# Second attention of a two-layer cross-attention and experts kernel: the shared experts' second product in token-major form

## The chip, the cores and the metric

One core of one Trainium2 chip. The metric is the device time of one execution in microseconds (us). Most executions of a kernel agree within 0.3%, and about 1% is what a comparison of medians of this kernel can tell from no change.

## What is computed

The input is 32 tiles of 128 tokens with 128 features. Two layers follow each other, each a cross-attention with a residual and a mixture of experts with a residual. The change touches the second layer alone. Its attention is a linear one (softmax over the 8 features of a head of queries and keys, then products with a summed key-value matrix); its experts' part has eight routed experts, of which each token takes two, and two shared experts that every token takes:

```
sh     = gelu(einsum('td,sdh->sth', xf, sW1) + sb1)        # s = 2 shared experts, h = 512
shared = (einsum('sth,shd->std', sh, sW2) + sb2).mean(axis=0)
gates  = xf @ rW + rb                                      # top 2 of 8, softmax over the two
moe    = sum over the two chosen experts of w * (gelu(xf @ W1[e] + b1[e]) @ W2[e] + b2[e])
x      = x + shared + moe
```

xf is the layer norm of the residual stream after the attention. All arithmetic that matters here is float32; the routing's counts and ranks are products of bfloat16 zeros and ones.

## The kernel before

Each engine has one hand-written queue of instructions; semaphores (`S("name")`) tie them together. The order in each queue is the order of the source. The kernel runs through five stages: the first attention (to about 240 us), the first routed experts (to about 400), the second attention with the shared experts woven in (about 404 to 615), the second routed experts, and the additions of their results.

**Second attention.** The 32 tiles are done in eight groups of four (`NGRP` = 8, `GT` = 4). On TensorE the loop is `for u in range(NGRP + 2)` at L1775: iteration u has group u's attention, group u-1's routing and, between them, the two shared experts for earlier groups. The latter come as `fill(k, ...)`: `half(u, k)` (L1692) turns k = 0 to 15 into one half of a shared chunk, an even k an up product (`shared_up`), an odd k a down product (`shared_down`, L1714). A group has eight chunks (`NC1S` = 8: two experts, four slices of 128 hidden units), so there are 64 chunks in all; the first down product of group g stands at k = 11 of iteration g+1, its last at k = 9 of iteration g+2.

TensorE's order in iteration u: turn the normed input; fill 0, 1; queries; fill 2, 3; `expert_turned(u-1)` (turns `xa`, the input of the experts); fill 4, 5; `exps_turned(u)`; `logits(u-1)`; fill 6, 7; `values(u)` (the numerators `nums`, in banks 2 and 3); fill 8, 9; `column_sums(1, u-1)`; fill 10; `out_turned(u)`; fill 11; `ranks(1, u-1)`; fill 12; `project(u)`; `shared_turn(u-2)`; fill 13 to 15.

**The shared experts' second product.** The hidden activations `hS` lie with hidden units on the partitions and the group's 512 tokens along them. `shared_down` takes the weights (128 x 128) as the stationary operand and streams the 512 tokens, so the result is features by tokens, summed over eight chunks in bank 6. ScalarE's `shared_out` (L828 to 834) halves it, adds the bias (`sb2`, one value for each partition) and puts it into `yS`; `shared_turn` (L1717) turns it into token-major form in bank 7 with four transposes, and VectorE's `shared_add` (L1052) adds it to the residual stream `x_sb`.

**Routing.** For each group VectorE's `choose` (L886) picks two experts from the logits, `column_sums` and `ranks` (L1363, L1369) on TensorE count and rank the choices, VectorE's `sums` (L911) copies the column sums out of PSUM between them and `slots` (L928) makes row numbers; GpSimd scatters the rows (L554) and makes the inverse deviations (`inverse_std`, L529). For layer 1 column sums and ranks use bank 7 (`rank_bank`), which they share with the turned shared result. After the last group VectorE's `block_list` (L949) writes `e_i`, from which the sync queue (L445 to L458) fetches weights and rows for each block of the routed experts.

**ScalarE** in iteration u (L836 to L867): copy of the turned input; gelu(0); `keep_input(u-1)` (L664 into `xa`); gelu(2); exponentials of the queries (L847); copy of the turned `xa` into `xeT_all` (a call of `turned`); gelu(4); copy of the turned exponentials; gelu(6); normed input of the next group; gelu(8); `shared_out(u-2)`; gelu(10); copy of the turned output; gelu(12), gelu(14). Gelu and the exponential need different tables; the program that builds the instructions puts in ACT_TABLE_LOADs, which have the line of the activation that they precede.

**VectorE** in iteration u (L1299 on): bias and moments, query, additions of the first experts' results, `shared_add(u-3)`, logits and `choose` for u-1, `output(u)` (L1277, four long instructions), `sums`, `gates`, `slots` for u-1, residual and moments of u. The shared bias is summed once ahead of group 0 (`shared_bias`, L1239). `link` makes VectorE wait for the instruction before.

## Time and profile before

| what | value |
|---|---|
| median of 3 runs | 783.42 us (781.82 to 787.84) |
| the profiled execution | 779.32 us |
| its span in the trace | 777.3 us |
| TensorE busy | 685.8 us, 88% |
| VectorE busy | 465.3 us, 60% |
| ScalarE busy | 326.5 us, 42% |
| GpSimd busy | 382.0 us, 49% |
| shared down products, L1714 | 128 passes, 65.4 us |
| shared result on ScalarE, L833 | 8 of 687 ns |

How to read it: the busy shares are means over stages that have different limits. A float32 product is seen as two MATMUL passes. A pass's length in the timeline has a modelled end and overlaps with the next, so what a product costs is read from the start of one to the start of the next. PE is TensorE's matmul, PEld its weight load, DVE VectorE, ACT ScalarE, POOL GpSimd, SP SyncE.

### The profile page before, as it was taken

To read this page: it belongs to the slowest core of one execution; us is meant where nothing else is said; L and a number is where in the kernel's file an instruction comes from. 1 tells how busy PE (TensorE), PEld (TensorE's weight loads), DVE (VectorE), ACT (ScalarE), POOL (GpSimd) and SP (SyncE) were. 2 spreads that over 40 slices of the span, in tenths; PEclk is the share of its full clock that TensorE was granted. 3 is DMA by queue.
4 is the path that set the end of the run, shared out by engine and by line. 5 is a ranking of instruction groups with operands and counts; after the bars stand their busy time and mean duration, and the time that the engine had idled before them with its cause. 6 is when DMAs were issued, how large, how long until landed. Compare 5 with 4: busy or idle time off the path is not lost.

```text
span 777.3 us, 15729 instructions
## 1 busy us (share of the span) xinstructions
PE 685.8 (88%) x5140; PEld 505.9 (65%) x5140; DVE 465.3 (60%) x1348; ACT 326.5 (42%) x689; POOL 382.0 (49%) x502
## 2 busy tenths in 40 slices
PE   7989999999898968899878799999999689999990
PEld 3556666667666668788776445555544289999990
DVE  4556877787677667776547766667553423333326
ACT  3434455445333232222212466666764244444440
POOL 5213176566537624556561365555555425545552
PEclk9999999999889789999987899999999999999995
DMA  6811111221101567777663000000000578877669
GB/s 165 251 22 9 10 32 22 31 30 25 33 10 36 127 175 235 236 227 234 196 212 91 1 24 22 21 29 25 21 29 29 131 247 266 262 245 237 220 200 283
DMA packets 102119, 91.34 MB, mean 118 GB/s; under 512 B 52952, under 2 KB 85848, under 8 KB 101720
## 3 DMA queue, kind: packets, MB, share of 16 engines
q1 hardware_dynamic: 86375, 68.80, 32.5%
q0 software_dynamic: 8640, 17.84, 6.5%
q10 hardware_dynamic: 7025, 3.70, 1.8%
q8 instruction: 42, 0.69, 0.4%
q14 instruction: 37, 0.30, 0.1%
HBM read 69.13 MB, written 22.72 MB: 118 GB/s over the span
## 4 chain that ended last, share of the span: by engine, by line
PE 50%; DVE 18%; SPq 10%; issue 9%; POOL 4%; ACT 4%; DMA 4%; another core or an unknown queue 2%; POOLq 0%; DVEq 0%
PE pair L1356 26%; PE pair L1662 9%; PE pair L1359 7%; DVE sm L1119 3%; SPq L417 2%; POOL xs_sorted L554 2%; DVE smax L1115 2%; PE pair L1714 2%; PE pair L1462 2%; DMA xr<-xs_sorted 2%; ACT xa L664 2%; PE pair L1477 2%; SPq L431 1%; PE pair L1397 1%
## 5 line engine op out<-in xcount | busy, mean ns | idle before, releaser
L627 POOL DMA_INDIRECT y_tok<-ysb,xr x142 | 137.6, 969 | 141.0 <-DVE ysb L1035 104.4
L554 POOL DMA_INDIRECT xs_sorted<-xa,slot_i x128 | 130.6, 1020 | 92.8 <-DVE slot_i L942 58.3
L1356 PE MATMUL pair<-xT,w_all 128*128 128x256 f32 (+1 forms) x640 | 140.5, 364 | 0.0
L1356 PEld LDWEIGHTS pair<-xT,w_all 128*128 128x128 f32 x640 | 110.4, 197 | 10.0
L1662 PEld LDWEIGHTS pair<-w_all,hT 128*128 128x128 f32 x852 | 106.2, 192 | 7.6 <-issue 4.4
L1662 PE MATMUL pair<-w_all,hT 128*128 128x128 f32 x852 | 108.3, 275 | 3.0 <-DVE hT L1022 2.2
L1014 DVE COPY xT<-pair 128x256 f32<-128x256 f32 (+1 forms) x80 | 31.5, 393 | 107.1 <-PE pair L1359 80.9
L804 ACT ACTIVATE hT<-pair,w_all 128x256 f32<-128x256 f32 (+1 forms) x160 | 61.5, 449 | 79.0 <-PE pair L1356 78.5
L1115 DVE TENSOR_REDUCE smax<-pair 128x8 f32<-128x616 f32 x64 | 50.4, 787 | 31.4 <-PE pair L1356 31.1
L1356 PE MATMUL pair<-xeT_all,w_sh 128*128 128x512 f32 x128 | 69.0, 622 | 0.0
L800 ACT ACTIVATE hg<-pair,w_all 128x256 f32<-128x256 f32 (+1 forms) x80 | 31.7, 447 | 88.1 <-PE pair L1356 59.2
L821 ACT ACTIVATE hS<-pair,w_sh 128x512 f32<-128x512 f32 x64 | 43.8, 685 | 53.5 <-PE pair L1356 43.2
L1714 PE MATMUL pair<-hS,w_sh 128*128 128x512 f32 x128 | 65.4, 593 | 0.0
L1119 DVE TENSOR_TENSOR sm<-pair,smax 128x616 f32<-128x616 f32 x64 | 51.1, 799 | 2.2
L1359 PEld LDWEIGHTS pair<-cst,sm 128*128 128x128 f32 x320 | 35.6, 146 | 24.7 <-issue 24.7
L1359 PE MATMUL pair<-cst,xr 128*128 128x128 f32 x142 | 30.9, 289 | 22.9 <-DMA xr<-xs_sorted 8.5
L1359 PE MATMUL pair<-cst,sm 128*128 128x128 f32 x320 | 50.5, 290 | 0.2 <-issue 0.2
L1356 PE MATMUL pair<-hT,yS 32*128 32x308 f32 x192 | 38.7, 478 | 10.5 <-DVE sm L1119 9.6
L1022 DVE SCALAR_TENSOR_TENSOR hT<-pair,w_all,hg 128x256 f32<-128x256 f32 (+1 forms) x80 | 32.5, 447 | 19.1 <-PE pair L1356 11.4
L704 ACT ACTIVATE wide<-pair 128x384 f32<-128x384 f32 x64 | 24.4, 433 | 42.0 <-PE pair L1359 42.0
L533 POOL TENSOR_SCALAR ve<-mv 128x4 f32<-128x4 f32 x32 | 7.7, 241 | 64.0 <-DVE mv L1070 62.6
L1714 PEld LDWEIGHTS pair<-hS,w_sh 128*128 128x128 f32 x128 | 23.0, 190 | 23.7 <-issue 21.2
(197 smaller groups left out, 1125.1 us busy)
## 6 DMA issues: line engine op xcount, KB each, us to landing
w_all<-in_w SPq DMA_DIRECT2D x40, 578.0 KB
w_all<-in_w SPq DMA_DIRECT2D x40, 450.0 KB
xa<-y_tok SPq DMA_DIRECT2D x32, 256.0 KB, 4.2
xr<-xs_sorted SPq DMA_DIRECT2D x62, 130.0 KB
y_tok<-ysb,xr POOLq DMA_INDIRECT x142
xs_sorted<-xa,slot_i POOLq DMA_INDIRECT x128
out<-x_sb ACTq DMA_DIRECT2D x8, 256.0 KB, 3.3
xs_sorted<-in_pads SPq DMA_DIRECT2D x12, 130.0 KB, 3.9
```

The costliest lines, as they stand in the source:

```text
L554: g.indirect_dma_start(xs_dram[l], bass.IndirectOffsetOnAxis(ap=slot_i[:, i:i + 1], axis=0), xa[:, GT * c + j // TOPK, j % TOPK, :], None) ...
L627: g.indirect_dma_start(y_dram[l], bass.IndirectOffsetOnAxis(ap=xr[u % NXR][:, t, P:P + 1].bitcast(I32), axis=0), ysb[u % NYB][:, t, :], None)\
L800: s_.activation(hg[k][:, c, 0:n], src, ACT.Silu, bias=w[:, bcol + c:bcol + c + 1])\
L804: s_.activation(hT[k][:, c, 0:n], src, ACT.Gelu, bias=w[:, bcol + c:bcol + c + 1])\
L821: s_.activation(hS[i % 4][:], bank[4 + i % 2][:], ACT.Gelu, bias=w_sh[:, col:col + 1])\
L1022: v.scalar_tensor_tensor(hT[k][:, c, 0:n], chunk(bank[2 * k + 1], c, BLK)[:, 0:n], w[:, bcol + c:bcol + c + 1], hg[k][:, c, 0:n], ALU.add, ...
L1115: link(v.reduce_max(smax[ab][:].rearrange("q (b h) -> q b h", b=2), score(ab), AX.X))
L1119: v.tensor_tensor(sm[ab][:, 0:SPAN].rearrange("q (b h k) -> q b h k", b=2, k=NK), score(ab), smax[ab][:].rearrange("q (b h) -> q b h", b=2 ...
L1356: return mm(out_, l_, r_, start=True, stop=True)
L1359: return nc.tensor.transpose(out_, in_, ident)
L1662: last = mm(bank[4 + k][:, t * P:(t + 1) * P], hT[k][:, c, t * P:(t + 1) * P], chunk(w, nu + c, P), start=(c == 0), stop=(c == nc_ - 1))
L1714: mm(bank[6][:], w_sh[:, wd:wd + P], hS[i % 4][:], start=(c == 0), stop=(c == NC1S - 1))\
```

## The change

The shared down product swaps its operands: for each chunk and each of the four tiles the activations are stationary and the weights stream, so that the result is tokens by features, in bank 6 or 7 in turn by group. `shared_turn` and `shared_out` go; `shared_add` reads the bank itself, halves and adds it, and adds the bias, which now is a row of 128 on every partition, inside `w_sh`. Column sums and ranks of layer 1 move to bank 2, one of the numerators' banks, so `column_sums` moves behind `out_turned`, and `values(u)` waits for the slots of group u-2. On ScalarE the copy of `xeT_all` moves ahead of the exponential. The routed stage waits for the shared additions of groups 0 to 6.

```
--- before.py
+++ after.py
@@ -49,7 +49,7 @@
 B1 = UP + F1
 W0C = B0 + 2 * NC0 + P
 W1C = B1 + NC1 + P
-WSC = NSH * B1 + NSH * NC1 + NSH
+WSC = NSH * B1 + NSH * NC1 + NSH * P
 WMAX = max(W0C, W1C)
 NWB = 5
 NXR = 8
@@ -238,7 +238,7 @@
         w_all = sb("w_all", [P, NWB * WMAX])
         w_blk = [w_all[:, i * WMAX:(i + 1) * WMAX] for i in range(NWB)]
         w_sh = sb("w_sh", [P, WSC])
-        sb2 = sb("sb2", [P, 1])
+        sb2 = w_sh[:, NSH * (B1 + NC1):NSH * (B1 + NC1) + P]
         cst = sb("cst", [P, K_N])
         wa = sb("wa", [P, W_N])
         wq0, wk0, wv0, wo0 = (wa[:, i:i + P] for i in (W_Q0, W_K0, W_V0, W_O0))
@@ -385,7 +385,7 @@
             return 7 if u == U_LAST else 6
 
         def rank_bank(l):
-            return bank[6 + l]
+            return bank[6 - 4 * l]
 
         def chunk(w, c, n):
 
@@ -825,14 +825,6 @@
                     act.wait_ge(S(done), u + 1)
                     copy_out(dst, bank[0][:]).then_inc(S(name), 1)
 
-                def shared_out(u):
-                    act.wait_ge(S("sdown_step"), NC1S * (u + 1))
-                    if u == 0:
-                        act.wait_ge(S("sb2_ready"), 1)
-                    after(act, S("sT_done"), u - 1)
-                    s_.activation(yS[u % 2][:], bank[6][:], ACT.Identity, bias=sb2[:], scale=1.0 / NSH)\
-                        .then_inc(S("sy_ready"), 1)
-
                 for u in range(-1, NGRP + 2):
                     if live(u):
                         turned("xnT_done1", xnT4, "xnT_ready1", u)
@@ -842,11 +834,11 @@
                     gelu(u, 2)
                     if u == NGRP + 1:
                         tail_rows(1, 5)
+                    if live(u - 1):
+                        turned("xeT_done1", xeT_all[:, (u - 1) * GT * P:u * GT * P], "xeT_ready1", u - 1)
                     if live(u):
                         act.wait_ge(S("f_sub"), u + 1)
                         s_.activation(e4, qb4, ACT.Exp).then_inc(S("f_exp"), 1)
-                    if live(u - 1):
-                        turned("xeT_done1", xeT_all[:, (u - 1) * GT * P:u * GT * P], "xeT_ready1", u - 1)
                     gelu(u, 4)
                     if u == NGRP + 1:
                         tail_rows(1, 6)
@@ -858,8 +850,6 @@
                     if live(u + 1):
                         norm_input(1, u + 1, xn4)
                     gelu(u, 8)
-                    if live(u - 2):
-                        shared_out(u - 2)
                     gelu(u, 10)
                     if live(u):
                         turned("oT_done1", oT4, "oT_ready1", u)
@@ -1050,9 +1040,11 @@
                         low_counts(l)
 
             def shared_add(g):
-                dve.wait_ge(S("sT_done"), g + 1)
-                xg = x_sb[:, GT * g:GT * (g + 1), :].rearrange("p t d -> p (t d)")
-                v.tensor_tensor(xg, xg, bank[7][:], ALU.add).then_inc(S("sx_added"), 1)
+                dve.wait_ge(S("sdown_step"), NC1S * (g + 1))
+                xg = x_sb[:, GT * g:GT * (g + 1), :]
+                link(v.scalar_tensor_tensor(xg, bank[6 + g % 2].rearrange("p (t d) -> p t d", d=P), 1.0 / NSH, xg,
+                                            ALU.mult, ALU.add))
+                v.tensor_tensor(xg, xg, sb2.unsqueeze(1).to_broadcast([P, GT, P]), ALU.add).then_inc(S("sx_added"), 1)
 
             def combine(l, g, c, done):
 
@@ -1238,9 +1230,9 @@
 
             def shared_bias():
                 dve.wait_ge(S("ws_in"), 16)
-                sbc = NSH * (B1 + NC1)
-                link(v.tensor_tensor(sb2[:], w_sh[:, sbc:sbc + 1], w_sh[:, sbc + 1:sbc + 2], ALU.add))
-                v.tensor_scalar(sb2[:], sb2[:], 1.0 / NSH, None, ALU.mult).then_inc(S("sb2_ready"), 1)
+                sbc = NSH * (B1 + NC1) + P
+                link(v.tensor_tensor(sb2, sb2, w_sh[:, sbc:sbc + P], ALU.add))
+                link(v.tensor_scalar(sb2, sb2, 1.0 / NSH, None, ALU.mult))
 
             def attention1():
 
@@ -1709,18 +1701,12 @@
                     s, k = divmod(c, NC1)
                     pe.wait_ge(S("sh_ready"), i + 1)
                     if c == 0:
-                        after(pe, S("sy_ready"), g)
+                        after(pe, S("sx_added"), g - 1)
                     wd = s * B1 + UP + k * P
-                    mm(bank[6][:], w_sh[:, wd:wd + P], hS[i % 4][:], start=(c == 0), stop=(c == NC1S - 1))\
-                        .then_inc(S("sdown_step"), 1)
-
-                def shared_turn(u):
-                    pe.wait_ge(S("sy_ready"), u + 1)
-                    pe.wait_ge(S("slots"), NCH + min(u + 2, NGRP))
-                    after(pe, S("sx_added"), u)
                     for t in range(GT):
-                        last = turn(tile(bank[7], t), tile(yS[u % 2], t))
-                    last.then_inc(S("sT_done"), 1)
+                        last = mm(tile(bank[6 + g % 2], t), tile(hS[i % 4], t), w_sh[:, wd:wd + P],
+                                  start=(c == 0 and t == 0), stop=(c == NC1S - 1 and t == GT - 1))
+                    last.then_inc(S("sdown_step"), 1)
 
                 def turns(src, name):
                     for t in range(GT):
@@ -1758,6 +1744,8 @@
                     pe.wait_ge(S("eT_ready1"), u + 1)
                     if u == 0:
                         pe.wait_ge(S("kvm_ready"), NGRP)
+                    if u > 1:
+                        pe.wait_ge(S("slots"), NCH + u - 1)
                     for t in range(GT):
                         last = one(nums[:, t, 0:KVC], tile(eT4, t), kvm_all[:, (GT * u + t) * KVC:(GT * u + t + 1) * KVC])
                     last.then_inc(S("num_done1"), 1)
@@ -1802,22 +1790,20 @@
                     if u == 0:
                         keep_clock(3, 5)
                     fill(8, 9)
-                    if live(u - 1):
-                        after(pe, S("sx_added"), u - 2)
-                        column_sums(1, u - 1)
                     fill(10)
                     if live(u):
                         out_turned(u)
+                    if live(u - 1):
+                        column_sums(1, u - 1)
                     fill(11)
                     if live(u - 1):
                         ranks(1, u - 1)
                     fill(12)
                     if live(u):
                         project(u)
-                    if live(u - 2):
-                        shared_turn(u - 2)
                     fill(13, 14, 15)
             attention1()
+            pe.wait_ge(S("sx_added"), NGRP - 1)
             pe.wait_ge(S("emap"), 2)
             routed(1)
 
@@ -1845,7 +1831,7 @@
     w1 = np.concatenate([i[M1 + "W1"], halves(i[M1 + "W2"]), cols(i[M1 + "b1"]), rows(i[M1 + "b2"])], axis=2)
     ws = np.concatenate([np.concatenate([i[M1 + "sW1"][s], halves(i[M1 + "sW2"])[s]], axis=1) for s in range(NSH)]
                         + [cols(i[M1 + "sb1"])[s] for s in range(NSH)]
-                        + [cols(i[M1 + "sb2"])[s] for s in range(NSH)], axis=1)
+                        + [np.broadcast_to(i[M1 + "sb2"][s][None, :], (P, P)) for s in range(NSH)], axis=1)
     wa = np.concatenate([i[n][:, None] for n in (A0 + "bq", A0 + "bk", A0 + "bv", A1 + "bv")]
                         + [i[A0 + "Wk"].T, i[A0 + "Wq"].T, i[A0 + "Wv"].T, i[A0 + "Wo"].T, i[M0 + "Wg"].T]
                         + [i[A1 + "Wq"].T, i[A1 + "Wk"].T, i[A1 + "Wv"].T, i[A1 + "Wp"].T, i[M1 + "rW"]], axis=1)
```

## Rows read from the trace of the kernel before

**Rows 1.** The chain of waits, group five to six; columns: start us, us, engine, tile, line.

```profile
530.14 0.81 PE pair L1356 x8
...
537.84 0.86 PE pair L1714 x2
...
542.93 1.45 POOL xs_sorted L554
...
546.97 1.57 ACT xa L664 x3
```

**Rows 2.** Timeline, all engines: start us, us, engine, line, operation, out<-in, count [idle before <-releaser].

```profile
540.76 0.60 PE L1359 MATMUL pair<-cst,yS 128*128 128x128 f32 x4
...
541.20 1.02 PE L1714 MATMUL pair<-hS,w_sh 128*128 128x512 f32 x2
...
542.06 1.02 PE L1356 MATMUL pair<-xeT_all,w_sh 128*128 128x512 f32 x2
```

**Rows 3.** Timeline of TensorE in the routed experts' stage.

```profile
703.02 1.95 PE L1662 MATMUL pair<-w_all,hT 128*128 128x128 f32 x16
704.81 0.38 PE L1359 MATMUL pair<-cst,xr 128*128 128x128 f32 x2
```

**Rows 4.** The page's costliest groups: busy us, mean ns of one, idle before.

```profile
L1662 PEld LDWEIGHTS pair<-w_all,hT 128*128 128x128 f32 x852 | 106.2, 192 | 7.6 <-issue 4.4
```

**Rows 5.** Timeline, all engines, from the kept input to the turned exponentials.

```profile
547.68 1.02 PE L1714 MATMUL pair<-hS,w_sh 128*128 128x512 f32 x2
...
548.47 0.69 DVE L1269 TENSOR_TENSOR wide<-wide,fmax 128x512 f32<-128x512 f32 x1
...
548.59 0.66 PE L1359 MATMUL pair<-cst,xa 128*128 128x128 f32 x4
...
549.12 1.28 ACT L847 ACT_TABLE_LOAD   x1
...
550.42 0.63 ACT L847 ACTIVATE wide<-wide 128x512 f32<-128x512 f32 x1
...
550.96 0.58 ACT L661 ACTIVATE xeT_all<-pair 128x512 f32<-128x512 f32 x1
...
551.68 0.63 PE L1359 MATMUL pair<-cst,wide 128*128 128x128 f32 x4 [0.71 <-ACT xeT_all L661]
```

**Rows 6.** Timeline of the same place one group in, where no gelu has run.

```profile
438.80 0.62 ACT L847 ACTIVATE wide<-wide 128x512 f32<-128x512 f32 x1
...
439.64 0.60 ACT L661 ACTIVATE xeT_all<-pair 128x512 f32<-128x512 f32 x1 [0.22 <-PE pair L1359]
...
440.38 0.64 PE L1359 MATMUL pair<-cst,wide 128*128 128x128 f32 x4 [0.78 <-ACT xeT_all L661]
```

**Rows 7.** Timeline around the column sums and the ranks.

```profile
557.65 0.19 PE L1356 MATMUL pair<-ones_b,oh 128*64 128x1 bf16 x1
...
557.77 1.13 PE L1356 MATMUL pair<-xeT_all,w_sh 128*128 128x512 f32 x2
...
559.21 0.28 DVE L915 CAST csum<-pair 64x128 bf16<-64x128 f32 x1
...
560.71 0.19 PE L1374 MATMUL pair<-oh,tri 128*128 128x64 bf16 x1
```

**Rows 8.** Timeline around the shared bias, then VectorE's group of a 128x128 sum.

```profile
419.42 0.15 DVE L1242 TENSOR_TENSOR sb<-w_sh 128x1 f32<-128x1 f32 x1
...
419.68 1.41 DVE L1061 TENSOR_TENSOR x_sb<-x_sb,xa 128x512 f32<-128x512 f32 x2
...
L1035 DVE TENSOR_TENSOR ysb<-ysb,xr 128x128 f32<-128x128 f32 x18 | 5.3, 292 | 0.6
```

**Rows 9.** VectorE's group of the shared addition, then its wait for group three's logits.

```profile
L1055 DVE TENSOR_TENSOR x_sb<-x_sb,pair 128x512 f32<-128x512 f32 x8 | 5.4, 677 | 4.5 <-PE pair L1359 4.5
...
508.82 0.19 DVE L1273 TENSOR_TENSOR lg<-pair,rb 128x32 f32<-128x32 f32 x1 [2.05 <-PE pair L1356]
```

**Rows 10.** The chain of waits behind the last ranks: the block list's last instruction.

```profile
611.08 0.26 DVE e_i L989
```

58 lines of the change are left out of this document (23 added, 35 removed).

## The prediction

> **What bounds the kernel now.** I read the page's busy table first: TensorE is the busiest engine over the whole span, so the tempting view is that every matmul saved is time saved. The chain of waits for the second attention says otherwise, and it is the view to read next. Followed through one group of four tiles it never stays on TensorE. The logits' products (L1356) release VectorE's choice of experts and its output arithmetic; that releases the turning of the output (L1359), one shared down product (L1714) and the ranks; these release the slots; the slots release three scatters on GpSimd, of which the last shown takes 1.45 us; behind them come the inverse deviation and ScalarE's copies into `xa` (L664), and the next group's exponential and logits [rows 1]. So the stage is a loop of latencies that closes once per group, not a queue of matmuls. The timeline of that group shows how near the two are: `xa` is ready at 546.97 + 1.57 = 548.54 us [rows 1], TensorE ends its work ahead of the turning of `xa` at 547.68 + 0.86, also 548.54 [rows 2, 5], and a little later it stands idle for 0.71 us until ScalarE has delivered the exponentials and `xeT_all` [rows 5]. The reader is to see in the brackets behind that row who ends the wait. After the last group the chain goes from the last ranks through slots and block list to `e_i`, ready at 611.08 + 0.26 us [rows 10]; from there the sync queue starts the experts' blocks. What delays the last ranks delays everything behind, since no block can be fetched before.
>
> **The change part by part.**
>
> *The down products.* 64 chunks. Before, each is one product of 512 columns, seen as two passes: 541.20 to 542.06, 0.86 us [rows 2]. After, each is four products of 128 columns with the activations stationary, eight passes. The routed down product has that form: 16 passes from 703.02 to 704.81, 1.79 us, 0.112 us a pass [rows 3], so 0.895 us a chunk, +0.035 us. That row's activations are stationary too, but it finishes one tile before the next, while the new code goes round four tiles of a bank; no row shows that order. Bounds: 0.107 us a pass, as the wide passes stream (0.86 / 8), so no loss at all; and 0.192 us of load in the open ahead of each pass [rows 4], 8 x (0.192 + 0.107) = 2.39 us a chunk. I take 0.112, the nearest row. Over 64 chunks TensorE gets 2.2 us more work.
>
> The row shows loads of 0.192 us each at a pitch of 0.112 us, so they lie beside the passes [rows 3, 4]. The Trainium skill, "TensorE: Matmul & The Clock Gate", Part 3, "The mechanism", says that a weight load overlaps matmuls in flight only when it goes to other row groups. All loads here take the full 128 rows, so by that rule none of the 512 would hide and the change would be a disaster; by the row it costs 0.035 us a chunk. The trace contradicts the rule for this form, and I go by the trace.
>
> *The turned result goes.* Eight groups of four transposes (540.76 to 541.20, 0.44 us [rows 2]) leave TensorE, 3.5 us; eight 512-wide copies leave ScalarE. But the transposes stand behind the projection, in the stretch of TensorE's queue that ends at the turning of `xa`. There TensorE arrives just in time; arriving 0.44 us earlier, it waits for `xa`. ScalarE's copy stood after `gelu(u, 8)`, outside the loop. Neither saving is worth time in this loop.
>
> *Column sums behind the turned output.* They must go there, because their bank is now the numerators'. Before, they ran in the shadow of VectorE's output arithmetic (TensorE waited for that anyway); now they lie between turned output and ranks, on the loop. One takes 557.65 to 557.77, 0.12 us [rows 7], and the down product between them and the ranks adds 0.035 us: 0.155 us for each of groups 1 to 7, 1.1 us. Do the ranks then wait for VectorE's copy of the sums? That copy takes 0.28 us [rows 7] and starts some 0.25 us after the sums were issued, and the down product covers 0.895 us: about 0.35 us to spare. Bounds for the position: 0 (if the wait for the output shrinks elsewhere) to 0.65 us (cover gone: 0.12 plus all of sums and copy).
>
> *ScalarE's order.* Before: gelu, table load (1.28), exponential (550.42), copy of `xeT_all` (550.96 to 551.54), and TensorE goes on at 551.68 [rows 5]. The table load needs nothing and starts at 549.12, when gelu ends, even before VectorE has subtracted the maximum (548.47 + 0.69) [rows 5]. After: the copy comes first and must wait for the turning of `xa`, which ends at 548.59 + 0.66 = 549.25 [rows 5], an idle of some 0.15 us that the table load used to fill. Then copy to 549.87, table load to 551.17, exponential (0.63) to 551.82, TensorE 0.13 us later: 551.95 instead of 551.68. +0.27 us in each of groups 2 to 7, 1.6 us. The logits, whose input would be ready sooner, stand behind that same turning of the exponentials in TensorE's queue and gain nothing. In group 1 no gelu has run yet, no table has to be loaded, and the exponential (438.80) ran while TensorE turned `xa`; the copy follows at 439.64 and TensorE goes on at 440.38 [rows 6]. After the change the exponential starts only when the copy is done: +0.6 us, its whole length. Bounds for each group: 0.1 (if the table load is put ahead of the copy, so that only the order of two short instructions changes) and 0.63 (nothing of the exponential hidden).
>
> *VectorE.* The shared addition becomes two instructions, 0.68 us more each time [rows 9]; it stands in front of the logits, where VectorE waited for 2.05 us in group 3 [rows 9] and longer in the groups without results to add. Hidden; if that cover went, 0.7 us for each of the groups concerned. The bias grows from one column to 128: 0.29 us an instruction as a 128x128 sum [rows 8] and one link more. It starts at 419.42 and what follows started at 419.68 [rows 8]; 0.29 + 0.29 + 0.04 for each link give 420.04, +0.35 us, and VectorE is on the chain there. Bounds: 0.1 to 0.4.
>
> *The end of the stage.* In the last iteration nothing is turned out or exponentiated, and column sums and `fill(10)` only change places; four down products ahead of the ranks cost 0.14 us. The two added pieces of the last shared additions come after the block list, while the sync queue is still fetching the first rows; the final wait on `sx_added` is met before they land. The 254 columns added to the shared weights' load (0.13 MB) land hundreds of microseconds early. The numerators' new wait for slots of two groups before was met one iteration earlier. No DMA is moved past another.
>
> Sum: 1.1 + 1.6 + 0.6 + 0.35 + 0.14 = +3.8 us. The profiled execution took 779.32 us (span 777.3 and 2.0 around it), which gives 783.1. It lies 4.1 us under the median of the runs, 783.42, to which the same sum is added: 787.2 us.
>
> **The rivals.**
>
> *TensorE's side of the loop decides: not slower.* TensorE and `xa` meet at 548.54 from both sides [rows 1, 5], so it may be that TensorE's own work sets the pace. Then a group costs 0.12 + 5 x 0.035 - 0.44 = -0.15 us up to that meeting, and the later waits would have to absorb the rest. Up to the last ranks six turned results go (2.6 us) and 57 down products are added (2.0 us): -0.6 us, 782.8. It decides wherever ScalarE is no longer what TensorE waits for at the exponentials. Against it: the 0.71 us of idle there exists already, and ScalarE's new order lengthens it.
>
> *The ranks wait for VectorE.* Between column sums and ranks stood two shared products and the output's turning; now one down product. If VectorE's copy comes later than the 0.35 us to spare, every group pays the difference. With 0.5 us on seven groups: +3.5 on top, 790.7. For it: the sums now reach VectorE when it has just finished its output and its queue holds nothing ahead; so the cover should do.
>
> *The loads don't hide.* 512 loads instead of 128 in these chunks, 384 x 0.192 us = 74 us if all are in the open [rows 4], 861 us before anything else is added. The rule quoted above would give this. It decides if going round four tiles keeps a load from starting during the pass before it; the routed product speaks against it in 852 passes [rows 3, 4].
>
> **How the numbers follow.** Forecast 0.70, TensorE's side 0.17, waiting ranks 0.10, open loads 0.03. What a measurement of this kernel can tell from no change is about 1%, 7.8 us. The forecast's +3.8 us and both first rivals are inside that. Slower by over 1%: the open loads, a third of the waiting ranks, and 0.03 for a forecast with its terms at their upper ends: 0.09. Faster by over 1% would need more than twice all that leaves TensorE: 0.02. Range: from the rival at 782.8 less 2 for the scatter of medians (runs from 781.82 to 787.84) to the waiting ranks at 790.7 with 1 above it: 780.5 to 791.5.
>
> **What would show it.** Passes of L1714's successor at a pitch of 0.112 us; TensorE's idle ahead of the turned exponentials up from 0.71 to about 0.9 us or more, with the exponential as releaser; the stretch from one turned output to the next some 0.4 us longer; ranks without a wait for the copy of the sums; `e_i` about 3.8 us later in the span, and the same distance from there to the end. I am wrong if the groups come closer together, if the idle ahead of the exponentials shrinks, or if the down products take more than 1 us a chunk.

## The result and the profile after

The kernel with the change takes 788.57 us in the median of seven runs (786.14 to 794.78), the kernel before 781.82 us in seven (779.89 to 787.84). The ratio is 1.0082 with the interval 1.0044 to 1.012: 6.4 us more, between 3.4 and 9.4. That is inside what was called no change, and it is nevertheless a loss that the interval separates from none. The kernel before had its median at 783.42 us when the forecast was made, so the forecast's +3.8 us is to be set against +6.4. The profiled execution took 787.66 us (span 785.6) against 779.32 us (777.3).

The page's busy table and two of its costliest groups, kernel after (busy us, mean ns of one, idle before):

```profile
PE 689.3 (88%) x5492; PEld 540.7 (69%) x5492; DVE 472.3 (60%) x1356; ACT 321.1 (41%) x681; POOL 384.2 (49%) x502
...
L1707 PEld LDWEIGHTS pair<-w_sh,hS 128*128 128x128 f32 x512 | 67.3, 196 | 28.4 <-issue 20.4
...
L1707 PE MATMUL pair<-w_sh,hS 128*128 128x128 f32 x512 | 70.0, 281 | 4.7 <-ACT hS L821 4.6
```

L1707 is the new down product, the place of L1714. All 512 passes are there, and their loads of 196 ns lie beside them. Now the chain of waits through the same group as in [rows 1] (start us, us, engine, tile, line):

```profile
542.98 0.66 PE pair L1351 x4
543.64 0.12 PE pair L1348
543.76 1.09 PE pair L1707 x8
544.85 0.03 PE pair L1366
...
549.06 1.47 POOL xs_sorted L554
...
553.10 1.58 ACT xa L664 x3
554.73 0.66 PE pair L1351 x4
...
557.13 0.88 issue
558.01 0.66 PE pair L1351 x4
```

The loop is the same as before: output turned, ranks, slots, three scatters (the third 1.47 us, before 1.45), `xa`, exponentials, logits. Two things are new in it. Between the turned output and the ranks (L1366) stand a column sum of 0.12 us and a whole down product of 1.09 us. And the turning of the exponentials at 558.01 comes behind 0.88 us of idle where [rows 5] had 0.71. The timeline of that second place, all engines:

```profile
554.73 0.66 PE L1351 MATMUL pair<-cst,xa 128*128 128x128 f32 x4 [0.17 <-ACT xa L664]
...
555.42 0.60 ACT L661 ACTIVATE xeT_all<-pair 128x512 f32<-128x512 f32 x1 [0.17 <-PE pair L1351]
...
556.03 1.28 ACT L841 ACT_TABLE_LOAD   x1
...
557.33 0.63 ACT L841 ACTIVATE wide<-wide 128x512 f32<-128x512 f32 x1
...
558.01 0.66 PE L1351 MATMUL pair<-cst,wide 128*128 128x128 f32 x4 [0.88 <-issue]
```

It is the order that the prediction wrote down for ScalarE: copy, table load, exponential, each at once behind the other, and TensorE 0.05 us after the last. The releaser is printed as "issue"; the exponential's end at 557.96 says who it is, and in the four groups ahead of this one the same 0.88 us is printed with `ACT wide L841`.

**Where the time went.** I call the stretch from the start of group 0's reciprocal (VectorE, `frec`) to the start of the block list's last instruction (`e_i`) the stage. The two ends, kernel after, timeline of VectorE:

```profile
429.09 0.96 DVE L1278 RECIPROCAL frec<-pair 128x128 f32<-128x128 f32 x1 [0.20 <-PE pair L1348]
449.12 0.95 DVE L1278 RECIPROCAL frec<-pair 128x128 f32<-128x128 f32 x1
...
585.41 0.95 DVE L1278 RECIPROCAL frec<-pair 128x128 f32<-128x128 f32 x1
...
618.59 0.25 DVE L979 CAST e_i<-erow 1x192 int32<-1x192 f32 x1
```

and the same of the kernel before:

```profile
426.59 0.96 DVE L1286 RECIPROCAL frec<-pair 128x128 f32<-128x128 f32 x1 [0.20 <-PE pair L1356]
445.74 0.95 DVE L1286 RECIPROCAL frec<-pair 128x128 f32<-128x128 f32 x1
...
578.56 0.95 DVE L1286 RECIPROCAL frec<-pair 128x128 f32<-128x128 f32 x1
```

Before, the stage ends at 611.08 [rows 10], so it took 184.49 us; after, 618.59 - 429.09 = 189.50 us. Of the 8.3 us by which the two spans differ, 5.0 lie in the stage, 0.3 in the bias ahead of it, 0.8 behind it, and the other 2.2 ahead of it in unchanged code, where single executions scatter by more than that (group 0's reciprocal starts between 421.75 and 434.63 us in the runs below that went on one chip). So the stage is read apart from the run's time from here on, in three pieces: group 0 to 1 (19.15 us before, 20.03 after), the six distances from group 1 to group 7 (132.82, 136.29), and from there to `e_i` (32.52, 33.18). The six are the clean measure: in one kernel they agree within 0.1 to 0.2 us where nothing disturbs them. A group costs 0.58 us more. Counted from its own reciprocal, group five has the ranks at 4.41 us before and 4.75 after, the turning of `xa` at 14.46 and 14.80, the turning of the exponentials at 17.55 and 18.08, and the next reciprocal at 22.16 and 22.73: 0.34 us come in ahead of the ranks, 0.19 between the two turnings and 0.04 behind them. (The profile of one run below, a2, fell in an execution disturbed by a lower clock, so its stage isn't read.)

### The profile page after: what moved, and what is told of

The parts are those of the page before. It is cut to its first block, busy times and chain, and to the rows that moved or that the text cites. A ratio compares the mean times of both kernels' runs of the same rounds, so it can differ in the third digit from the quotient of the medians.

```text
span 785.6 us, 16425 instructions
## 1 busy us (share of the span) xinstructions
PE 689.3 (88%) x5492; PEld 540.7 (69%) x5492; DVE 472.3 (60%) x1356; ACT 321.1 (41%) x681; POOL 384.2 (49%) x502
## 4 chain that ended last, share of the span: by engine, by line
PE 55%; DVE 19%; issue 8%; SPq 6%; POOL 4%; ACT 3%; DMA 3%; another core or an unknown queue 1%; DVEq 1%; POOLq 0%
PE pair L1348 28%; PE pair L1654 10%; PE pair L1351 8%; DVE sm L1111 3%; DVE smax L1107 3%; PE pair L1707 3%; PE pair L1454 2%; POOL xs_sorted L554 2%; PE pair L1469 2%; DMA xr<-xs_sorted 1%; SPq L452 1%; ACT xa L664 1%; DVE bns L1057 1%; SPq L445 1%
## 5 line engine op out<-in xcount | busy, mean ns | idle before, releaser
L1348 PE MATMUL pair<-xT,w_all 128*128 128x256 f32 (+1 forms) x640 | 143.1, 369 | 0.0
L1348 PEld LDWEIGHTS pair<-xT,w_all 128*128 128x128 f32 x640 | 112.6, 202 | 10.3
L1654 PE MATMUL pair<-w_all,hT 128*128 128x128 f32 x852 | 110.3, 278 | 10.2 <-DVE hT L1012 10.2
L1654 PEld LDWEIGHTS pair<-w_all,hT 128*128 128x128 f32 x852 | 107.8, 195 | 15.6 <-issue 12.5
L1707 PEld LDWEIGHTS pair<-w_sh,hS 128*128 128x128 f32 x512 | 67.3, 196 | 28.4 <-issue 20.4
L1707 PE MATMUL pair<-w_sh,hS 128*128 128x128 f32 x512 | 70.0, 281 | 4.7 <-ACT hS L821 4.6
L664 ACT ACTIVATE xa<-x_sb,nmr,rstd 128x256 f32<-128x256 f32 x64 | 33.1, 592 | 11.6 <-POOL nmr L536 11.6
```

The source lines that it names most:

```text
L664: return s_.activation(dst, src, ACT.Identity, bias=nmr4[w][:, t:t + 1], scale=rstd4[w][:, t:t + 1])
L1348: return mm(out_, l_, r_, start=True, stop=True)
L1654: last = mm(bank[4 + k][:, t * P:(t + 1) * P], hT[k][:, c, t * P:(t + 1) * P], chunk(w, nu + c, P), start=(c == 0), stop=(c == nc_ - 1))
L1707: last = mm(tile(bank[6 + g % 2], t), tile(hS[i % 4], t), w_sh[:, wd:wd + P], start=(c == 0 and t == 0), stop=(c == NC1S - 1 and t == GT - 1))
```

## The experiments

Each short diff is against the kernel named with it. "Before" and "after" are the two kernels of this case. The table gives the ratio of times with its interval and the stage in its pieces; what each says follows below.

| run | ratio to before | stage | 0 to 1 | six groups | 7 to `e_i` |
|---|---|---|---|---|---|
| before | 1 | 184.49 | 19.15 | 132.82 | 32.52 |
| after | 1.0082 (1.0044 to 1.012) | 189.50 | 20.03 | 136.29 | 33.18 |
| e1 after, ScalarE's old order | 1.0031 (0.9996 to 1.0067) | 188.72 | 20.28 | 135.28 | 33.16 |
| e4 before, ScalarE's new order | 1.0031 (0.999 to 1.0071) | 186.64 | 20.03 | 134.12 | 32.49 |
| e2 after, sums early | 1.0018 (0.9986 to 1.005) | 187.51 | 20.04 | 134.52 | 32.95 |
| e3 after, both | 0.9971 (0.9938 to 1.0003) | 183.76 | 19.52 | 131.29 | 32.95 |
| e5 after, four idle turns | 1.0051 (1.0022 to 1.0081) | 190.39 | 20.81 | 136.40 | 33.18 |
| e6 before, third scatter late | 1.0002 (0.9973 to 1.0031) | 183.03 | 19.58 | 131.46 | 31.99 |
| e7 e3, third scatter late | 1.0112 (1.0057 to 1.0166) | 193.63 | 19.58 | 141.27 | 32.78 |
| e8 after, third scatter late | 1.0079 (1.0044 to 1.0114) | 189.15 | 20.03 | 136.95 | 32.17 |
| a2 after again, other chip | 1.0082 (1.0054 to 1.011) | not read | | | |
| e11 e3 again, other chip | 0.9965 (0.9936 to 0.9994) | 183.77 | 20.15 | 130.39 | 33.23 |
| e9 e3, third scatter in the gap, other chip | 0.9968 (0.9941 to 0.9995) | 182.84 | 20.29 | 130.37 | 32.18 |
| e10 before, third scatter in the gap, other chip | 0.9944 (0.9921 to 0.9967) | 181.56 | 20.38 | 129.21 | 31.97 |

**ScalarE's order, from both sides.** e1 gives the changed kernel the old order, e4 gives the old kernel the new one.

```
# e1, against after                          # e4, against before: the opposite
-  if live(u - 1):
-      turned("xeT_done1", ..., u - 1)
   act.wait_ge(S("f_sub"), u + 1)
   s_.activation(e4, qb4, ACT.Exp)
+  if live(u - 1):
+      turned("xeT_done1", ..., u - 1)
```

e1_order_back:


> The changed kernel with ScalarE's two instructions back in their old order. The stretch from group 0's reciprocal to the block list's last instruction took 184.49 us before and 189.50 us after the change, and one group 22.16 and 22.73 us. Loop theory: the order costs 0.19 us in each of groups 2 to 7 and 0.6 in group 1, so the stretch falls by 1.7 us to 187.8 and a group to 22.54. TensorE theory (its own work sets the pace): its work is unchanged, so the stretch stays at 189.5 and a group at 22.7.


e4_order_alone:


> The kernel before with nothing changed but ScalarE's order (the copy of xeT_all ahead of the exponential). Stretch from group 0's reciprocal to the block list's last instruction: 184.49 us in the kernel before. My prediction's working: +0.27 in each of groups 2 to 7 and +0.6 in group 1, 186.7 us. By the trace of the changed kernel (0.19 a group) 186.2. TensorE theory: unchanged, 184.5. A rival in which the copy ahead lets TensorE start the logits sooner: below 184.5.

The six groups: e1 takes 1.01 us off the changed kernel (0.17 each), e4 puts 1.30 on the old one (0.22 each). Forecast were 0.27. The order alone leaves the last piece as it was (32.49 against 32.52), as it must, since nothing is exponentiated there. The timeline of e1 at the place shown above:

```profile
550.77 0.66 PE L1351 MATMUL pair<-cst,xa 128*128 128x128 f32 x4 [0.17 <-ACT xa L664]
...
551.31 1.28 ACT L839 ACT_TABLE_LOAD   x1
552.60 0.63 ACT L839 ACTIVATE wide<-wide 128x512 f32<-128x512 f32 x1
553.14 0.58 ACT L661 ACTIVATE xeT_all<-pair 128x512 f32<-128x512 f32 x1
...
553.86 0.63 PE L1351 MATMUL pair<-cst,wide 128*128 128x128 f32 x4 [0.68 <-ACT wide L839]
```

In the old order the table load starts when gelu ends, without the turned `xa`: 3.09 us from the turning of `xa` to that of the exponentials, 3.28 in the changed kernel. What the exponentials hang on differs too: in the old order they follow the end of ScalarE's own work on `xa`, in the new one TensorE's turning of it. This will matter below. The +0.6 us forecast for group 1 is seen best from group 0's reciprocal. Group 1's exponentials are turned 13.79 us behind it before, 14.21 after and 14.20 in e4: the order costs 0.42 us there. From that turning to group 1's reciprocal it takes 5.36 us before and 5.82 after. But all the other profiles read here have 5.73 to 5.83, e3, e6, e7 and e10 with the old order among them, so some 0.4 of the piece's 0.88 us is a peculiarity of the one profile of the kernel before and no cost of the change; e4's close hit (186.64 us against 186.7) has this luck in it. The piece also depends on the granted clock: with the new order 20.03 us at 0.85 and 20.81 at 0.75 (e5), with the old one 19.58 at 0.85 (e7) and 20.28 at 0.75 (e1). That is 0.45 and 0.53 us for the order at equal clocks, and it is why e1's expectation for the whole stage was missed by this piece, not by its groups.

**The column sums' place.** e2 takes the ranks' bank away from the numerators, so that the sums can stand ahead of the shared products again; e3 is e1 and e2 together.

```
# e2, against after (e3: with e1's edit too)
-  return bank[6 - 4 * l]
+  return bank[6 - 5 * l]          # ranks: bank 1 in layer 1
...
-  if u > 1:
-      pe.wait_ge(S("slots"), NCH + u - 1)   # in values
...
+  after(pe, S("slots"), NCH + u if u else 0)   # in project
...
+  if live(u - 1):
+      column_sums(1, u - 1)
   fill(10)
...
-  if live(u - 1):
-      column_sums(1, u - 1)
```

e2_sums_early:


> The changed kernel with the layer's column sums and ranks in bank 1, so that the column sums stand ahead of fill(10) again (the projection then waits for the slots, which costs it some 0.1 us). Loop theory: column sums and the load in the open behind them leave the loop, 0.34 - 0.10 = 0.24 us a group on seven groups, the stretch falls by 1.7 us to 187.8. TensorE theory: the same instructions, only in another place, no change (189.5) or a little more by the projection's wait (190).


e3_both:


> Both edits on the changed kernel: what stays of the change is the down product's form, the turned result that went, and VectorE's sum. Loop theory: only the narrow down product ahead of the ranks stays on the loop, 0.1 us a group; the stretch falls by 3.4 to 186.1 us, a group to 22.3, the whole kernel to within 0.3% of the kernel before. If the narrow down products as such are what costs (TensorE theory), the stretch stays above 188.5 us and the ratio to before near 1.008.

With the new order, e2 takes 1.77 us off the six groups, 0.29 each, where 0.155 was forecast for the sums' place. The timeline of the changed kernel shows what the place costs:

```profile
542.98 0.66 PE L1351 MATMUL pair<-cst,wide 128*128 128x128 f32 x4 [0.75 <-DVE wide L1282]
...
543.57 0.19 PE L1348 MATMUL pair<-ones_b,oh 128*64 128x1 bf16 x1
...
543.69 0.97 PEld L1707 LDWEIGHTS pair<-w_sh,hS 128*128 128x128 f32 x8
543.69 1.16 PE L1707 MATMUL pair<-w_sh,hS 128*128 128x128 f32 x8
543.80 0.28 DVE L905 CAST csum<-pair 64x128 bf16<-64x128 f32 x1 [0.87 <-PE pair L1348]
...
544.68 0.19 PE L1366 MATMUL pair<-oh,tri 128*128 128x64 bf16 x1
```

From the turned output to the sums it takes 0.59 us, where the kernel before has 0.50 from the turned output to the down product; the sums 0.12; and the down product 0.99 us until the ranks start, where 0.895 was taken and the old wide product took 0.86. Together that is the 0.34 us. Inside the loop the same product takes 0.89 (the third line is the next one, in its own place):

```profile
548.66 0.86 PEld L1707 LDWEIGHTS pair<-w_sh,hS 128*128 128x128 f32 x7 [0.24 <-issue]
548.66 1.05 PE L1707 MATMUL pair<-w_sh,hS 128*128 128x128 f32 x8
...
549.55 0.60 PE L1351 MATMUL pair<-cst,hT 128*128 128x128 f32 x4
```

Count the loads: eight stand with the first product, seven with the second, whose first load ran under the work before it. Behind the column sum, whose one column offers no cover, the first of the eight lies in the open. The copy of the sums, 543.80 to 544.08, is done 0.6 us before the ranks: they don't wait for it.

e3 is the surprise. e1 gave 1.01 us over six groups and e2 1.77, 2.78 if they added up; together they give 5.00, and 5.90 in e11, the same kernel on the other chip (e3 had one group held for 0.9 us, e11 none). The stage comes to 183.76 and 183.77 us, shorter than before the change. These lines of its timeline show what else changed:

```profile
522.67 0.96 POOL L554 DMA_INDIRECT xs_sorted<-xa,slot_i  x1 [0.30 <-issue]
523.02 0.66 DVE L1252 TENSOR_TENSOR x_sb<-x_sb,bias 128x512 f32<-128x512 f32 x1
...
528.37 0.60 PE L1351 MATMUL pair<-cst,xa 128*128 128x128 f32 x4
530.93 0.63 PE L1351 MATMUL pair<-cst,wide 128*128 128x128 f32 x4 [0.22 <-issue]
```

The third scatter takes 0.96 us and not 1.45 or 1.47. In the kernel before, the group shown in [rows 1]:

```profile
542.89 0.66 DVE L1260 TENSOR_TENSOR x_sb<-x_sb,bias 128x512 f32<-128x512 f32 x1
542.93 1.45 POOL L554 DMA_INDIRECT xs_sorted<-xa,slot_i  x1 [0.30 <-issue]
```

There VectorE's addition of the bias, two operands from SBUF, starts just ahead of the scatter and covers its start; the scatter ends 0.83 us after it. In the changed kernel it is the same (9.10 us after the group's reciprocal, scatter 9.13). This distance of 0.83 to 0.84 us from the addition's end to the scatter's stands in the groups 1 to 6 of both kernels, and as 0.82 to 0.84 in those of e1, e4 and e5, whether the scatter takes 1.27 or 1.47 us, and where no addition falls on it (group 7) it takes 0.96. In e2 and e3 the ranks are early, so the scatter starts at 8.83, while the projection waits for the slots and the bias addition comes only at 9.17: it finds the scatter started. This bears on a rule of the Trainium skill, "SBUF — State Buffer", "Who interferes with whom": a VectorE instruction with two inputs in SBUF contends with a GpSimd instruction that reads SBUF, and issue order decides who blocks. The trace agrees that GpSimd pays when the addition is first (1.45 against 0.96 us); VectorE's addition takes 0.66 us in either order, so that it would block in its turn isn't seen. The same section infers that such an addition leaves the writing of DMA descriptors alone; if that is what the scatter's instruction does on GpSimd, the 1.45 us speak against it. That the port is the cause is the rule's word, no run here shows it.

With the scatter short and the ranks early, ScalarE starts on `xa` 0.81 us sooner after the reciprocal than in the changed kernel (11.86 against 12.67 us). e2 can use little of it: in the new order the exponentials wait for the turning of `xa`, which now stands behind TensorE's own work (it starts 2.67 us after `xa`, in the changed kernel 2.13) and comes only 0.28 us sooner. In e3, with the old order, they follow `xa` itself: 5.22 us from the start of `xa` to the turned exponentials in before, e1 and e3 alike, and the whole 0.8 reaches the next group, although the turning of `xa` itself is no sooner than in the kernel before (14.53 against 14.46 us). Each of the two moves hid part of what the other cost.

**Does the turned result's removal pay?** e5 puts four transposes a group into the changed kernel behind the projection, whose result is read by nobody.

```
# e5, against after, behind project(u)
+  if 2 <= u < NGRP:
+      for t in range(GT):
+          turn(tile(bank[0], t), ident)
```

e5_dummy_turns:


> The changed kernel with four transposes of the identity put back where the turned shared result stood (iterations 2 to 7, result unused): 0.44 us more work for TensorE each time, no new wait. Loop theory: TensorE was 0.36 us early or waiting at the turning of xa, so 0 to 0.1 us a group comes through, the stretch 189.5 to 190.1 us. TensorE theory: all of it comes through, 6 x 0.44 = 2.6 us, stretch 192.1 us.

Five of the six added turns lie in the six distances, 2.2 us of TensorE's work, and cost 0.11 us there; the sixth lies in the last piece and costs nothing (33.18 us both). The turning of `xa` moves by 0.10 us in its group, the next group by 0.05. TensorE's side doesn't decide here. The piece from 0 to 1 is 0.8 us longer, and no turn was added there. The windows line of e5 for it has the stretch, its length, busy us and count of PE, PEld, VectorE, ScalarE and GpSimd, then the granted clock, the DMA share and GB/s:

```profile
421.75:442.56 20.81, 15.63 (x60) 10.62 (x60) 13.84 (x44) 9.45 (x18) 5.79 (x11) 0.75 0.00 1
```

The clock was granted at 0.75 there, against 0.85 in the changed kernel.

**The third scatter moved behind the inverse deviations.** If the scatters are what the loop waits for, leaving two instead of three ahead of the inverse deviation should give the long one back.

```
# e6 against before, e7 against e3, e8 against after
-  scatter(1, u - 2, 3, NPS)
+  scatter(1, u - 2, 2, NPS)
...
-  scatter(1, u - 1, 0, 3)
+  scatter(1, u - 1, 0, 2)
```

e6_two_scatters_before (the 44 ns in it are a slip for 0.44 us):


> The kernel before with two instead of three of a group's scatters ahead of the kept input's inverse deviation on GpSimd (the third goes with the rest, behind it). Loop theory: the slots-to-xa part of the loop loses one scatter of 1.3 us, but TensorE's side meets xa within 0.1 us, so little of it shows: TensorE's 44 ns turned results and its down products then set the pace at the turning of xa, and what is gained is what TensorE idles there, 0 to 0.2 us a group, at most 1.5 us in the stretch (183 to 184.5). GpSimd theory (the rest of the scatters then come late and hold the gates back): slower, up to 1 us a group.


e7_two_scatters_e3:


> The changed kernel with both positions back (order and column sums) and two scatters ahead. Now TensorE's side has 0.44 us less per group than before and so can use a shorter way from slots to xa. Loop theory: from 186.1 us for both positions alone it falls by about 0.3 us a group to some 184.0, at or below the kernel before with two scatters by 0 to 1 us. TensorE theory: no change against both positions alone.


e8_two_scatters_after:


> The changed kernel as it is, with two scatters ahead. Loop theory: the way from slots to xa gets 1.3 us shorter and TensorE has 0.2 to 0.5 us of idle there to give back, so a group falls from 22.73 to 22.3 to 22.5 us and the stretch from 189.5 to 186.5 to 188. TensorE theory: nothing, 189.5.

e6 came out at the lower end of what was expected: its stage takes 183.03 us, 1.46 less than before. Three groups take 21.56 to 21.60 us instead of 22.1, two take 0.24 and 0.26 us more than in the kernel before. That is 0.2% of the time, which the ratio (0.9973 to 1.0031) can't tell from none. e7 lost 10 us where the stage was expected to gain. e8 lost 0.7 us over six groups where a gain was expected; with 1.0 us gained behind the last group its stage is 0.35 us shorter. What was expected inside the group is there in two of them: in e8 ScalarE starts on `xa` 0.95 us and the exponentials are turned 0.38 us sooner after the reciprocal, in e6 the latter 0.53 us sooner. In e7 nothing is gained on e3 (exponentials at 17.0 us in both): the turning of `xa` stays where TensorE's own work puts it, at 14.4 us. What eats the gain is a hold in front of the next reciprocal, here in the chain of waits of e7:

```profile
545.93 0.17 DVE high L899
546.10 1.15 another core or an unknown queue
...
547.27 0.97 DVE frec L1278
```

VectorE has chosen the experts by 546.10 and starts the reciprocal, whose input is a product long done, at 547.27. In e7 the hold is 1.1 to 1.2 us in five groups and 0.5 in the last, in e8 0.4 to 0.5 us in five and 0.2 in the last, in e6 0.2 to 1.1 us in three. ScalarE stands at about the same time (timeline of e7):

```profile
547.27 0.96 DVE L1278 RECIPROCAL frec<-pair 128x128 f32<-128x128 f32 x1 [1.17 <-remote]
547.31 0.69 ACT L821 ACTIVATE hS<-pair,w_sh 128x512 f32<-128x512 f32 x1 [1.29 <-PE pair L1348]
```

The brackets name no engine of this core that was still at work. What holds the two is open; I have no run that shows it, and e9 below speaks against scatters that merely run until late. In e3 VectorE was held once too, for 0.9 us in front of the logits between the last two reciprocals, with three scatters ahead.

The holds are 6.2 of e7's ten us. Another 3.1 lie between the turned output and the ranks of three groups, where TensorE ran at a lower clock. The windows line of e7 that holds the first of them (columns as in the line of e5; the clock stands third from the end):

```profile
502.00:524.00 22.00, 20.83 (x129) 16.71 (x129) 13.44 (x50) 13.04 (x22) 12.60 (x19) 0.92 0.08 25
```

In a window of its own, 504 to 506 us has a granted clock of 0.50, which is the lower level (1.2 GHz); ahead of it TensorE had been idle for 1.61 us in front of the turned output, because VectorE was held. From the turned output to the ranks it then takes 2.58 us instead of e3's 1.39. Idle alone doesn't settle it: in two other groups of e7 TensorE idled for 1.63 us at the same place and the clock stayed.

**The third scatter in the gap, and the two main kernels again.** VectorE leaves a hole between the two statistics of a group, and GpSimd can take the third scatter between its two inverse deviations.

```
# e9 against e3, e10 against before
-  scatter(1, u - 1, 0, 3)
+  scatter(1, u - 1, 0, 2)
   ... the first inverse deviation, as it stands
+  if live(u - 1):
+      scatter(1, u - 1, 2, 3)
```

a2_change_again:


> The changed kernel once more. The stretch from group 0's reciprocal to the block list's last instruction is a chain with fixed durations and comes out at 189.5 us within 0.3; what lies ahead of it (429.1 us in the first profile, 426.6 before the change) differs from run to run, between 421 and 434 us in the profiles so far, so it is no part of the change. Ratio to the kernel before 1.004 to 1.010. If the change had slowed the stages ahead, group 0's reciprocal would come at 428.5 or later again.


e11_both_again:


> The changed kernel with both positions back (ScalarE's order, column sums ahead of fill(10) in bank 1), once more: stretch 183.8 us within 0.3, ratio to the kernel before 0.994 to 1.000. If the first run's gain was scatter, the ratio is above 1.000.


e9_third_in_gap_e3:


> As the one before, and on GpSimd the third scatter goes between the two inverse deviations, into a gap of its queue, so that the last scatters are not later than with three ahead. Theory 1 (late scatters hold VectorE's reciprocal back, as with two scatters ahead): nothing is late now, a group takes 21.6 us and the stretch 183 to 184 us, since TensorE's side sets the turning of xa. Theory 2 (two scatters ahead as such cost, by what follows on TensorE): a group stays at 22.8 us or more, stretch above 190 us.


e10_third_in_gap_before:


> The kernel before with GpSimd's third scatter between the two inverse deviations. With two scatters ahead three of six groups took 21.6 us and three 22.0 to 22.4. Theory 1: all groups take 21.6 us, the stretch falls from 184.49 to 181 to 182 us, ratio to before 0.995 to 0.998. Theory 2: the groups stay mixed, stretch 183 us.

These four ran on another chip, where the kernel before takes 747.71 us. The change has the same ratio there, 1.0082, and e3 nearly the same, 0.9965 against 0.9971. e10 is the best kernel of the study: 743.28 us against 747.71, 0.9944 (0.9921 to 0.9967). Its stage, 181.56 us, is what was expected of it. Its groups take 21.5 us on average instead of 22.1 (the kernel before was profiled on the first chip only), none is held, and its timeline shows the three scatters without a long one, the third behind the first deviation:

```profile
510.78 1.03 POOL L554 DMA_INDIRECT xs_sorted<-xa,slot_i  x1 [4.67 <-DVE slot_i L944]
...
512.12 0.96 POOL L554 DMA_INDIRECT xs_sorted<-xa,slot_i  x1 [0.30 <-issue]
...
513.53 0.57 POOL L533 TENSOR_SCALAR ve<-mv 128x4 f32<-128x4 f32 x1 [0.44 <-DVE mv L1072]
...
516.31 1.08 POOL L554 DMA_INDIRECT xs_sorted<-xa,slot_i  x1 [0.47 <-issue]
```

GpSimd's first small operation takes 0.57 us instead of 0.23, beside the same addition of the bias: the overlap is still there, but a short instruction pays less. On e3, where the bias addition no longer covers a scatter's start, the same edit gains nothing in the six groups (130.37 against 130.39): ScalarE starts on `xa` 0.07 us sooner, and the turning of `xa` stays at 14.52 us, where TensorE's own work puts it. Behind the last group it gains 1.05 us. Nothing of the change is in e10, so what helped was never the down products' form.

e9 was also to tell whether late scatters hold VectorE back. Its last scatter of a group comes later against the reciprocal than in e7, and nothing is held:

```profile
504.08 0.96 POOL L554 DMA_INDIRECT xs_sorted<-xa,slot_i  x1 [0.31 <-issue]
...
504.30 0.95 DVE L1280 RECIPROCAL frec<-pair 128x128 f32<-128x128 f32 x1
```

In e7 the last scatter ends at 545.90, and the reciprocal starts only at 547.27. So their lateness by itself isn't the cause.

## Why the prediction came out as it did

The forecast, no measurable change with a small loss, was right in kind; +3.8 us was too little by 2.6 in the medians. By its steps, in the profiled executions:

- **The down products' form: right.** The pitch is 0.89 us a chunk inside the loop, 0.895 forecast, and all but a few loads lie beside passes. The rival of the open loads is out. The rule of the Trainium skill against which the row was weighed doesn't hold for these loads: 512 passes with full-height loads show the same as the 852 of [rows 4]. The same section also lets a load go ahead into "the background weight buffer", which the prediction left out and which would allow what is seen.
- **The turned result and its copy: right.** In e5 five turns come back for 0.11 us. That is the changed kernel alone. In e3, where TensorE sets when `xa` is turned, their absence may be worth more; that wasn't tried. The copy of the result wasn't put back alone either.
- **Column sums behind the turned output: right in kind, the term that was mis-sized.** The prediction put 0.155 us a group, "it lies between turned output and ranks, on the loop"; measured are 0.34 from the output to the ranks (3.05 to 4.75 us after the reciprocal, against 3.05 to 4.41 before). Its first part, 0.12 for the sums, was right. The mis-sized part is the 0.035 for the down product behind them, which measured 0.13: it was priced as in the middle of a stream, and stands behind a product of one column, with its first load in the open (0.99 us in the timeline instead of 0.895; the chain of waits has 1.09). Another 0.09 is a gap ahead of the sums that wasn't forecast. In e2 the ranks are back at 4.44 us.
- **ScalarE's order: right, a bit high.** 0.27 forecast, 0.17 and 0.22 measured (e1, e4), 0.19 between the two turnings of the changed kernel. The changed order is as drawn, and idle ahead of the turned exponentials is 0.88 where "about 0.9 or more" was said. Group 1: +0.6 forecast, since the whole exponential would be in the open; 0.42 measured at the turned exponentials.
- **VectorE's longer shared addition: right inside the loop, not behind it.** It takes two instructions of 0.68 and 0.69 us, and VectorE still waits for the logits behind it, in group five for 1.86 us. But in the last group the second one, whose two operands both come from SBUF, runs beside GpSimd's inverse deviation, which is on the chain there:

```profile
595.27 0.69 DVE L1047 TENSOR_TENSOR x_sb<-x_sb,w_sh 128x512 f32<-128x512 f32 x1
...
595.65 0.40 POOL L533 TENSOR_SCALAR ve<-mv 128x4 f32<-128x4 f32 x1
```

  GpSimd's instruction takes 0.40 us where the kernel before has 0.23. In e3 the next one takes 1.31 instead of 1.04, in e11 the first 0.79. "Hidden" was put at nothing here and is 0.2 to 0.6 us, once.
- **The bias: right.** From the last addition to the kept values to the first of `x_sb` 0.38 us before and 0.70 after, +0.32 for the forecast's 0.35.
- **The end of the stage:** 0.3 forecast from group 7 to `e_i` (0.155 and 0.14), 0.66 measured. Of it 0.53 is there at the last turning of `xa` (14.01 and 14.54 us after the reciprocal), made of the ranks' 0.35 and the 0.17 that GpSimd loses beside VectorE; 0.13 lies behind it, where 0.14 was forecast. With the sums back, e2 and e3 leave 0.43 of the 0.66 and e11, the same kernel as e3, 0.71: what GpSimd loses differs.
- **Ranks waiting for the sums' copy: out.** It is done 0.6 us ahead of them.

Per group 0.155 + 0.27 = 0.425 forecast, 0.58 measured; times six 2.55 and 3.47. That the two are so near is in part luck, since the sums' place was put too low and the order too high (0.34 and 0.19 measured). With 0.42 instead of 0.6 for group 1, 0.66 instead of 0.3 behind group 7 and 0.32 for the bias, the parts make 4.9 us; the two profiles differ by 5.3, and the other 0.46 is what the profile of the kernel before has less than all others behind group 1's turned exponentials. The median's 6.4 (3.4 to 9.4) holds both, and in the other runs the stage and the median agree to within some 2 us either way. Of the signs that were named, one isn't there: the distance from `e_i` to the end was to stay the same and grew by 0.8 us, which nothing here explains. The ends of the range are rounded outwards and inwards: 782.8 - 2 is 780.8 and 790.7 + 1 is 791.7, where 780.5 and 791.5 were written; the result lies inside either.

What the prediction did not see at all is how its two main terms hang together. It took each delay as an amount to add. The runs show that each is worth more when the other is gone, because they stand on two branches (the exponentials on ScalarE's side, the turning of `xa` on TensorE's) and the later one hides the other. And it read the third scatter's 1.45 us in [rows 1] as a given length, where a third of it could go: a neighbour's start decides between 1.45 and 0.96. e3 compared with before, at the same positions in a group, shows this, with the change's other parts in place: ranks 4.44 and 4.41, third scatter starting at 8.83 and 8.80, then `xa` at 11.86 and 12.33 and the next group at 21.71 and 22.16. Whether the old kernel would gain the same by a later bias addition alone wasn't tried; e10 gets it by moving the scatter.

## What to carry to other kernels

In a loop of latencies an edit is worth what it puts on or takes off the branch that arrives last, and two edits on different branches don't add up: price them together, and test each alone and both. Here the weight loads were hidden behind products of 128 columns and the first one was not behind a product of one column, so price a product by what stands ahead of it in the queue. Before taking an instruction's length on the chain as given, compare it with its siblings, and look at who started beside it where it is longer. A wait that looks hidden on one engine can still slow a neighbour: look for what the hidden instruction runs beside.

## What was not expected of the hardware

- The third scatter, of 128 rows, holds GpSimd for 0.96 us, but for 1.27 to 1.47 when an addition of 128x512 with both operands in SBUF starts before it; it then ends 0.83 us behind the addition.
- VectorE and ScalarE stand 0.2 to 1.2 us although their inputs are done (e6, e7, e8, once in e3). Late scatters alone don't do it (e9). Open.
- In three of e7's six held groups a lower clock followed the hold: 0.50 was granted from 504 to 506 us, behind 1.61 us of TensorE's idle, and what takes 1.39 us in e3 took 2.58. In two others, with 1.63 us of idle, it did not.
- The table load of 1.28 us is followed by its exponential 0.02 us later. The Trainium skill, "ScalarE: Activation LUTs", "What ACT_TABLE_LOAD costs", adds 1.38 us of drain to each switch; in the rows above none is seen: the load starts 0.01 us behind the copy ahead of it (555.42 + 0.60), and 557.33 is 1.30 us after 556.03.
- The second chip runs every kernel some 4% faster, and this stage no faster: the first five of the six distances agree to 0.02 us between e3 and e11 (21.62 to 21.88). That the two stages come to 183.76 and 183.77 us is chance, since e3's held group and e11's longer first and last pieces cancel. They reach the stage at 429.27 and 394.86 us. Of these 34.4 us, 14.7 are there at the first block list (260.7 and 246.0 us), ahead of the routed experts and their traffic, and 19.7 come behind it. Why isn't shown; the granted clock up to 230 us was 1.00 in e11 and 0.96 in e3. The ratios agree on both chips.
- The piece from group 0 to 1 follows the granted clock of that stretch: 20.03 us at 0.85 and 20.81 at 0.75 with the new order, 19.58 at 0.85 and 20.28 at 0.75 with the old one.
